# Adding the second pair of expert outputs with an accumulating DMA

## The reference

```python
weights, indices = jax.lax.top_k(scores, 4)          # 4 of 32 experts for each token
for e in range(32):
    out = swiglu(xf[tok], W1[e], W2[e], W3[e]) * w[:, None]
    y = y.at[tok].add(out)                           # four rows in all are added for each token
x = x + (y + z).reshape(B, S, D)                     # z: the shared expert
q = layernorm(x) @ Wq + bq                           # layer 1, first step of its attention
```

## Time and profile before

| what | value |
|---|---|
| median of the runs | 1439.91 us |
| the profiled execution, whole | 1438.93 us |
| its span in the trace | 1437.2 us |
| PE, DVE, ACT, POOL busy | 84%, 54%, 37%, 30% |
| mean rate of all DMA | 86 GB/s |
| G<-y_rows, 2048 KB, issue to landing, median | 10.3 us |

### The profile page before, as it was taken

How to read it: one execution, slowest core, us unless ns; L and a number is a source line. 1 busy time by engine, 2 the same in 40 slices (tenths; PEclk the granted TensorE clock), 3 DMA queues, 4 the chain that set the end, 5 groups by cost and what they waited for, 6 DMA issues and landing times. The chain is left out here.

```text
span 1437.2 us, 27370 instructions
## 1 busy us (share of the span) xinstructions
PE 1208.0 (84%) x8592; PEld 839.1 (58%) x8592; DVE 782.1 (54%) x2039; ACT 524.8 (37%) x1064; POOL 431.6 (30%) x560
## 2 busy tenths in 40 slices
PE   8889999475666519999999827799997999999998
PEld 4467777354554308877778613577773555455554
DVE  3257777554655415666656577488874433443431
ACT  4745555221122103444344226455552221222221
POOL 4321211045566544555545535122210000000000
PEclk9989999797788759999999959899998999999999
DMA  6199000115124365545444293000000000000000
GB/s 163 11 293 392 31 1 1 38 54 88 65 85 160 115 208 168 154 145 165 145 137 144 61 353 122 12 2 1 1 1 1 15 1 15 16 15 15 15 1 30
DMA packets 99297, 123.63 MB, mean 86 GB/s; under 512 B 32688, under 2 KB 74607, under 8 KB 99187
## 3 DMA queue, kind: packets, MB, share of 16 engines
q1 hardware_dynamic: 85363, 87.82, 20.2%
q0 software_dynamic: 13824, 34.38, 6.8%
HBM read 61.62 MB, written 64.72 MB: 88 GB/s over the span
## 5 line engine op out<-in xcount | busy, mean ns | idle before, releaser
L1741 PE MATMUL psA<-H,B 128*128 128x512 f16 x1024 | 223.5, 379 | 0.0
L1666 DVE SCALAR_TENSOR_TENSOR H<-psA,H 128x512 f16<-128x512 f32 x128 | 88.3, 690 | 208.3 <-ACT H L1709 208.3
L1422 POOL DMA_INDIRECT y_rows<-YB,pair x160 | 155.5, 972 | 143.3 <-issue 73.8
L1741 PEld LDWEIGHTS psA<-H,B 128*128 128x128 f16 x1024 | 100.2, 98 | 119.3
L1532 PE MATMUL psH<-W,XT 128*128 x640 | 168.5, 386 | 0.4 <-ACT XT L1434 0.4
L1709 ACT ACTIVATE H<-psA 128x512 f16<-128x512 f32 x128 | 76.4, 597 | 252.3 <-PE psA L1741 252.3
L879 ACT ACTIVATE PHT<-psT 128x512 f16<-128x512 f32 (+1 forms) x192 | 93.9, 521 | 120.1 <-PE psT L939 119.7
L820 DVE TENSOR_REDUCE mx<-psS 128x8 fp32r<-128x616 f32 x128 | 101.6, 795 | 53.8 <-PE psS L918 51.8
L827 DVE TENSOR_TENSOR PLT<-psT,PHT 128x512 f16<-128x512 f32 (+1 forms) x192 | 109.5, 597 | 26.2 <-ACT PHT L879 26.2
L1532 PEld LDWEIGHTS psH<-W,XT 128*128 128x128 f32 x640 | 110.6, 193 | 11.2 <-issue 2.4
L1434 ACT ACTIVATE XT<-psX 128x256 f32<-128x256 f32 x160 | 61.4, 384 | 143.8 <-PE psX L1515 110.3
(11 more groups left out here) (251 smaller groups left out, 2207.2 us busy)
## 6 DMA issues: line engine op xcount, KB each, us to landing
XG<-x_rows SPq DMA_DIRECT2D x160, 134.0 KB
y_rows<-zero_row SPq DMA_DIRECT2D x4, 4096.0 KB
G<-y_rows SPq DMA_DIRECT2D x7, 2048.0 KB, 10.3
x_rows<-zero_row SPq DMA_DIRECT2D x33, 134.0 KB, 5.9
X<-in_x SPq DMA_DIRECT2D x8, 512.0 KB, 8.3
QT<-in_w SPq DMA_DIRECT2D x1, 4096.0 KB
out_x<-OUT SPq DMA_DIRECT2D x8, 512.0 KB, 3.0
y_rows<-YB,pair POOLq DMA_INDIRECT x160
```

The costliest lines, as they stand in the source:

```text
L1422: pool.indirect_dma_start(y_rows[:, :], bass.IndirectOffsetOnAxis(ap=pair[u // HALF][:, u % HALF:u % HALF + 1], axis=0), YB[u][:], None, b ...
L1666: dve.scalar_tensor_tensor(out=H[layer][1][:, o], in0=psA[k % 4][:], scalar=0.0, in1=H[layer][0][:, o], op0=ALU.max, op1=ALU.subtract).the ...
L1741: last = pe.matmul(psA[k % 4][:], W[:, c, o * P:(o + 1) * P], src[part][:, c], start=n == 0, stop=n == 2 * n_in - 1)
```

## The change

The four rows of a token are handled as two pairs. SyncE fetches only the first pair of each token, 1 MB per macro in 2 KB pieces, into one of six buffers of half the size. When a fetch has landed, GpSimd issues a DMA of the second pair onto the same buffer with `accum_op=ALU.add`, so that the DMA engines read what stands in G and in `y_rows` and write the sum. VectorE waits for this second DMA (`paired`) and makes two additions instead of four. GpSimd issues the first three of these DMAs before its power(0), and the one of macro m+3 behind power(m). The fetch of macro 0 is no longer cut into halves. The buffers take as much room as before (3 x 16 KB and 6 x 8 KB per partition).

```diff
-GBUFS = 3
+GBUFS = 6
+PAIR = TOPK // 2
...
-        G = [space(st, "G", [P, MT, TOPK * D]) for _ in range(GBUFS)]
-        fetched = [sem("fetched") for _ in range(GBUFS)]
-        halves = [sem("halves") for _ in range(2)]
+        G = [space(st, "G", [P, MT, PAIR * D]) for _ in range(GBUFS)]
+        fetched, paired = ([sem(s) for _ in range(GBUFS)] for s in ("fetched", "paired"))
...
+        def rows_of(m, k):
+            return y_rows[m * MW * TOPK:(m + 1) * MW * TOPK, :].rearrange(
+                "(t p k) d -> p t (k d)", p=P, k=TOPK)[:, :, k * PAIR * D:(k + 1) * PAIR * D]
...
                 def fetch(m):
                     if m >= GBUFS:
                         sp.wait_ge(summed, m - GBUFS + 1)
-                    sp.dma_start(G[m % GBUFS][:], rows_of(m, 0, MT)).then_inc(fetched[m % GBUFS], 16)
-                for h in range(2):
-                    sp.dma_start(G[0][:, 2 * h:2 * h + 2, :], rows_of(0, 2 * h, 2 * h + 2)).then_inc(halves[h], 16)
+                    sp.dma_start(G[m % GBUFS][:], rows_of(m, 0)).then_inc(fetched[m % GBUFS], 16)
+                fetch(0)
...
+                def add_pair(m):
+                    pool.wait_ge(fetched[m % GBUFS], 16 * (m // GBUFS + 1))
+                    pool.dma_start(G[m % GBUFS][:], rows_of(m, 1), accum_op=ALU.add).then_inc(paired[m % GBUFS], 16)
+                for m in range(3):
+                    add_pair(m)
                 for m in range(MACROS):
                     q.power(pool, m)
+                    if m + 3 < MACROS:
+                        add_pair(m + 3)
...
-                def add_up(m, lo, hi):
-                    x = X[:, m * MT + lo:m * MT + hi, :]
-                    for k in range(TOPK):
-                        own.done(dve.tensor_tensor(x, x, G[m % GBUFS][:, lo:hi, k * D:(k + 1) * D], ALU.add))
                 for m in range(MACROS):
...
+                    dve.wait_ge(paired[m % GBUFS], 16 * (m // GBUFS + 1))
+                    x = X[:, m * MT:(m + 1) * MT, :]
+                    for k in range(PAIR):
+                        own.done(dve.tensor_tensor(x, x, G[m % GBUFS][:, :, k * D:(k + 1) * D], ALU.add))
                     dve.sem_inc(summed, 1)
                     q.stats(dve, m)
```

More of the change, by code:

```diff
@@ L666, in _ @@
             def _(sp):
-                def rows_of(m, lo, hi):
-                    return y_rows[(m * MT + lo) * P * TOPK:(m * MT + hi) * P * TOPK, :].rearrange(
-                        "(t p k) d -> p t (k d)", p=P, k=TOPK)
                 def fetch(m):
```

## The result

The changed kernel takes 1452.28 us (median of five, 1448.54 to 1456.31), the kernel before 1438.57 us in the same comparison: ratio 1.011, 95% interval 1.0078 to 1.0141. It is slower by 13.7 us; 10.8 us had been forecast. Inside combine, from the first fetch's issue to the next block's first copy on GpSimd, the profiled executions give 75.87 us before (829.56 to 905.43) and 86.68 us after, a difference of 10.8 us.

A forecast was written before the change was run, and what follows sets the result against it. DMA engines bound combine: from 832.0, 21.8 (first pairs) + 43.6 (second pairs) + 0.7 (wq) reach 898.1; additions and a 15.64 tail end at 916.2, +10.8, giving 1450.7 us. Own range 1446 to 1456; eight in ten 1427 to 1474.

The forecast's parts named there:

- The gain that the VectorE row offered: In combine, two of four additions per macro go, 4.97 to 2.49 us; VectorE alone would give 17.4 us.
- the sign: In combine's profile, VectorE waits for a transfer before nearly each macro, some 3 us, if the forecast holds.
- The pieces: First-pair fetches in combine: 2 KB runs instead of 4 KB move at 385 GB/s, 21.8 us for 8.39 MB.
- the lower of the two prices: GpSimd's time to issue an accumulating DMA: near 1 us in the forecast, the other price near 4 us.
- rival C: GpSimd becomes combine's bound, held 3.9 us per accumulating DMA: +4, or 1444 us; chance 10%.
- The end of the stage: From combine's last addition to the next stage's first copy on GpSimd: kept at 15.64 us.
- The accumulation: Eight 1 MB accumulating DMAs in combine cost two plain transfers' worth, 43.6 us, between bounds of 21.8 and 65.4.
- the engines stay full: DMA engines in combine never starve: after macro m's pair lands, power(m) takes some 7 us, two others still need 10.9.
- The first sum: VectorE's first addition in combine starts at 844 to 848 us instead of 834.6.
- not what is late: SyncE's six fetches without a wait in combine are read ahead of the pair that is added, so not late.
- Rival A: Accumulation in combine runs at a copy's rate, DMA ending at 876.3: -11.0, or 1428.9 us; chance 24%.
- The granted clock: TensorE's clock in combine stays at 1.00 after 862 us; its gaps grow under 1 us per macro, costed at nothing.

The follow-up runs named there:

- e4_no_second: Changed kernel without GpSimd's eight DMAs of the second pairs, VectorE adding behind the fetch: combine 57.49 us, ratio 0.9855 to the kernel before.
- e1_copy: Changed kernel with each macro's second DMA as a plain copy without the add: combine 70.95 us, ratio 0.9958 to the kernel before.
- e2_one_add: Changed kernel with one addition by VectorE per macro instead of two, transfers unchanged: combine 84.53 us, ratio 1.0045 to the kernel before.
- after_again: Changed kernel rerun with no edit, on another chip: combine 86.13 us, ratio 1.0096 to the kernel before.
- after_third: Changed kernel run a third time with no edit: combine 85.72 us, ratio 1.0061 to the kernel before.

## Why the prediction was right

**The bound and the mechanism** were right. The forecast put the last pair 68.5 us after the first fetch (898.1 against 829.56); it was summed from 905.25 on, 68.8 us after 836.49. From 2.44 us behind the first fetch to there the engines moved 16.83 MB at 254 GB/s, the rate that was forecast, and VectorE waits 3.4 to 3.5 us in front of macros 1 to 3 (some 3 had been named as the sign). The gain that the VectorE row offered is real (18.4 us in e4_no_second) and it is the DMA engines that take it back (e1_copy against the changed kernel, e2_one_add).

**The pieces.** 2 KB runs at 385 GB/s: measured 387 to 389. GpSimd's issue: 1.27 to 1.43 us, near the lower of the two prices, so rival C falls. The end of the stage: 15.64 expected, 15.44 us measured (923.17 against 907.73).

**The accumulation** was priced at two plain transfers, 43.6 us for eight. Measured alone it is 208 GB/s, 5.04 us each and 40.3 us for eight: 1.86 times the plain 2 KB transfer (387), 1.96 times the 4 KB one (408). The Trainium skill ("Collectives: The Full Stack", section "The bandwidth ceiling: the fold count and why AG ≠ RS ≠ AR") gives a reduce-scatter about half the rate of an all-gather because of its second source read; the trace agrees with the factor. That it is the second read and not the add itself no run here separates.

**A step that failed** hid behind this: "the engines stay full". In 897 to 901 us the share is 0.72 and the rate 121 GB/s: the DMA of macro 7 stands behind power(4), which ended at 896.7, 7.8 us after macro 4's pair had landed, while accumulations 5 and 6 needed 5.1 us each and had arrived by 899.2. The last transfer was issued at 896.62 and landed at 905.2, 8.6 us later. I had counted two outstanding transfers as 10.9 us of work at that moment; at the end, when no fetches share the engines, it was less, and issue and first byte came on top. Against 208 GB/s the hole is worth 1.7 us. The reruns have it too (155 and 168 GB/s over four microseconds, in 826 to 830 us of after_again and 822 to 826 us of after_third).

That the end still came where I had put it is luck. Alone an accumulation takes 5.04 us; beside fetches it takes 5.4 by my estimate (in 846.5 to 887.5 us 5.26 MB of accumulations ran beside 5.41 MB of fetches, the latter priced at 387 GB/s). Five of the one and three of the other make 42.0 us and not 43.6. So the price was 1.6 us too dear, the hole of 1.7 us was left out, and the two cancel.

**The first sum** was expected at 844 to 848 on the clock of before, that is 14 to 18 us after the first fetch, and came 19.3 us after it. The rate stays at that of fetches alone until 846 us, some 4 us behind the issue of the first accumulation, and then its packets share the engines with those of the fetches of later macros; the prediction had called these fetches "not what is late". While the DMA engines are the bound this costs nothing. Rival A's time was too good by 6 us: a copy's price gave 4.9 us (e1_copy) and not 11.0. The last sum ended 4.7 us later than rival A has it, as the engines weren't kept full there either, and the stretch behind it took 17.1 us and not 15.6.

**The other engines' pace.** TensorE's 4.69 us per macro is 4.31 when it has no gap. The granted clock was costed at nothing, since TensorE's gaps would grow "by under 1 us per macro". By the prediction's own 8.2 us for a macro in place of 6.97 they grow by 1.2. The clock did fall once in the changed kernel, as TensorE's timeline shows:

```profile
880.68 1.10 PE L213 MATMUL psX<-ident,XN 128*128 128x128 f32 x8 [1.12 <-ACT XN L452]
881.62 3.60 PE L490 MATMUL psQ<-XT,WQ 128*128 128x512 f32 x8
888.73 1.97 PE L213 MATMUL psX<-ident,XN 128*128 128x128 f32 x8 [3.52 <-ACT XN L452]
890.49 5.65 PE L490 MATMUL psQ<-XT,WQ 128*128 128x512 f32 x8
```

After a pause of 3.52 us the transposes take 1.97 us instead of 1.10: the granted clock is 0.50 (1.2 GHz) in 889 to 893. It was back at 1.00 by the end, and the stretch behind the last sum took 15.4 to 15.6 us in all three profiles of the changed kernel, so it stayed off the path, as assumed.

**The range.** The forecast's own range, 1446 to 1456 us, comes out as 1447 to 1458 when three plain shares of 8.39 MB are moved at 408 or at 346 GB/s as it says. The measured 1452.28 is in both.

**What is not accounted for:** 13.7 us measured against 10.8 in combine; the reruns (12.4 and 7.5 against 10.3 and 9.9) say scatter ahead of combine rather than a second cost.

## What to carry to other kernels

Work moved from a vector engine onto an accumulating DMA isn't free: weigh its price, here 1.9 plain transfers, against the idle time that the DMA engines have in the very stretch, and move only as much as fits. Issue it long before it is wanted: fetch, wait, issue and a slow transfer in a row came to 19 us before the first sum. Two macros of eight, which fit into the slack and were issued ahead, took 3.5 to 3.8 us off combine; all eight put 10 on it.

## What the runs showed of the hardware that was not expected

- A plain copy of these 2 KB runs from GpSimd's queue goes in packets of 3.9 KB (634 packets, 2.47 MB), the accumulating one in packets of 2.0 KB (824 packets, 1.65 MB). GpSimd holds its instruction 0.75 to 0.83 us for the copy and 1.27 to 1.46 us for the accumulation.
- Fetches and accumulations shared the engines by packets, not by time: 5.24 MB in 860 to 880 us were 2.62 MB of each, in 1322 and 1326 packets, at 39.3% and 70.4% of the engines' time.
- The busy share of the DMA engines reads 1.08 to 1.13 at 202 to 262 GB/s where accumulations run, alone or beside fetches, and 1.02 to 1.06 at 381 to 417 GB/s of plain traffic. The share shows that they are taken, not how much they deliver; that takes the rate beside it.
